# Cross-attention and routed feed-forward on one core: query tiles apart, projections to the last unit, and the output projection of three batches inside the last attention

## The chip, the core and the metric

The kernel runs on one core of a Trainium2 chip. Its engines are TensorE (PE, with its weight loads as PEld), VectorE (DVE), ScalarE (ACT), GpSimd (POOL) and SyncE (SP), each with a queue of its own that is worked off in order; they meet by semaphores. SP and POOL also issue the DMAs. What counts is the device time of one execution in microseconds, as the median of the runs.

## What is computed

Eight batches of 224 rows of 512, with 750 rows of context each. All in fp32.

```python
x = x + attention(layernorm(x), ctx)   # 16 heads of 32, bias on the scores, padding mask
    # q = n @ w_q.T + b_q ; k, v = ctx @ w_k.T + b_k, ctx @ w_v.T + b_v
    # attn = softmax(q k^T * SCALING + attn_bias, masked) ; out = (attn v) @ out_proj_w.T + out_proj_b
n = layernorm(x)
    # dists to 32 prototypes, w = softmax(-dists / t), top_w, top_i = top_k(w, 2), top_w normalised
    # h = B[top_i] n (rank 16) ; y = A[top_i] h + bias[top_i]
x = x + sum(top_w * y)
```

## The kernel before

Two stages, each a block of five queues: `weave` and `finish`.

**weave.** Matmuls of the projections are made in three passes with fp32r halves (hi·hi, lo·hi, hi·lo). A batch of attention has 32 **units**, one for each head and half of the query rows (`w` counts units over all batches, `u` within one, `UB` = 32). In unit `w` TensorE turns the first half of the probabilities (`turn(w, 0)`), makes the scores of unit `w + 2`, and turns the second half (`turn(w, 1)`). VectorE adds the bias and finds the maximum (L727) and copies one half of the turned probabilities (L737), ScalarE makes the exponential (L566) and copies the other half (L575). After every eight units (`u % 8 == 1`) TensorE weighs the values for a group of four heads (L930) and turns the inverse sums (L939); GpSimd has widened these (`widen`, L475). `output` writes the group's attention, SyncE stores it to `attn_t` in DRAM.

Between these pieces stand the projections of the next batch: 14 tiles of keys and values and two of queries, 216 **steps** (matmuls) in all. `step_shares` deals them out over the units up to `last`, in three pieces a unit (before and behind the scores, and behind the second turning), none in a unit that weighs. A tile goes to one of two PSUM banks `acc` in turn, and its first step waits until the tile two before is evacuated, by ScalarE (`high_tile`) and VectorE (`low_tile`). Query tiles use one staging buffer (`query_staging`), which is free when its DMA to DRAM is done. `X_AT` says in which units the normalised x of the next batch is turned by TensorE (L887) into `out_ps`, the bank that also holds the attention's output. GpSimd splits the context into halves (L466, L468).

In batch 7 (the last) nothing is left to project. There GpSimd loads and splits the three matrices of the second stage (`load_weights`, `split_weights`, units `CHUNKS_AT`), and at unit 25 the attended rows of batch 0 (`split_attended`, `add_output_bias`).

**finish.** Per batch: output projection (`project_out`, 24 matmuls of 512 columns into `big`), residual into `x1` (L1265), layer norm (`norm`, `deviation`, `normalise`), transposes (`transpose_y`, L1452), distances to the prototypes, top two and weights (`routing`, `routing_weights`), `down` (48 matmuls of 224 columns), the route widened and transposed (L1186, L1490), `gate`, `up` (24 matmuls) and `result`. A **turn** of its loop holds the second half of batch `b` with the first half of `b + 1` and the projection of `b + 2`. GpSimd splits the attended rows of the next batch and adds the output bias to its x.

## Time and profile before

| | us |
|---|---|
| median of 3 runs | 901.77 (899.92 to 902.45) |
| profiled execution | 899.01 |
| its span, first to last instruction | 896.8 |
| TensorE busy in the span | 848.1 (95%) |
| VectorE, ScalarE, GpSimd busy | 610.3, 502.0, 185.3 |

In the span the first batch's projections come first, with the exponential of the first unit at 52.6 us. Batches then follow every 85 to 86 us until 648.5, where the attention of batch 7 starts. Its last exponential starts at 707.6, the second stage has its first matmul at 714.98, and the last instruction is at 896.8. The mean granted clock of TensorE is 0.992 of full speed. A share of busy time over the whole span mixes these stages, so they are to be read one by one.

### The profile page before, as it was taken

What the parts mean: (1) busy time and instruction counts of PE and PEld (TensorE: products, weight loads), DVE (VectorE), ACT (ScalarE), POOL (GpSimd) and SP (SyncE); (2) the same over time, 40 slices, a digit from 0 to 9 for tenths busy, and PEclk for the clock granted to TensorE, in tenths of its full rate; (3) what the DMA queues carried; (4) which work ended last, traced back from release to release, by engine and by line L of the source; (5) the groups of instructions that cost most, each with busy time, mean ns of one, the idle gap of its engine ahead of it and who ended that gap; (6) DMA issues with size and microseconds to landing.
All of it is one profiled execution on the core that took longest, in us unless ns stands there. A gap on an engine that the chain in (4) does not pass through costs nothing. (4 is left out here: it accounts for less than half of the span.)

```text
span 896.8 us, 20533 instructions
## 1 busy us (share of the span) xinstructions
PE 848.1 (95%) x8016; PEld 751.9 (84%) x8016; DVE 610.3 (68%) x1459; ACT 502.0 (56%) x1066; POOL 185.3 (21%) x240
## 2 busy tenths in 40 slices
PE   6999999999999999999999999999988769999998
PEld 6789898988898889889988989898876647888886
DVE  6586776677666666776686668666678457666664
ACT  5246666665565655666666566666667515444442
POOL 0050112011211201120112011200067233334400
PEclk9999999999999999999999999999999979999999
DMA  8975654675467647565556565546587211222211
GB/s 258 285 161 142 169 148 110 167 173 142 114 165 175 147 110 177 142 143 148 143 134 160 142 155 123 141 108 157 135 200 183 61 51 43 62 62 64 71 30 43
DMA packets 79457, 119.87 MB, mean 134 GB/s; under 512 B 8517, under 2 KB 58797, under 8 KB 79362
## 3 DMA queue, kind: packets, MB, share of 16 engines
q1 hardware_dynamic: 76866, 109.91, 48.8%
q0 software_dynamic: 2496, 8.65, 3.4%
q8 instruction: 64, 1.05, 0.5%
q14 instruction: 31, 0.25, 0.1%
HBM read 79.25 MB, written 39.28 MB: 132 GB/s over the span
## 5 line engine op out<-in xcount | busy, mean ns | idle before, releaser
L566 ACT ACTIVATE score_sb<-score_sb,neg_max 112x750 f32<-112x750 f32 x256 | 236.3, 923 | 74.2 <-DVE neg_max L727 72.4
L727 DVE CUSTOM_DVE_ANT_0 score_sb<-score_ps,neg_bias 112x750 f32<-112x750 f32 x256 | 239.4, 935 | 44.0 <-PE score_ps L906 43.3
L915 PE MATMUL prob_ps<-ident,score_sb 112*125 112x112 f32 x1536 | 248.7, 270 | 8.6 <-ACT score_sb L566 8.0
L915 PEld LDWEIGHTS prob_ps<-ident,score_sb 112*125 112x125 f32 x1536 | 229.9, 188 | 29.7 <-ACT score_sb L566 14.2
L575 ACT ACTIVATE probs_sb<-prob_ps 125x336 f32<-125x336 f32 x256 | 114.7, 448 | 170.5 <-PE prob_ps L915 168.2
L737 DVE COPY probs_sb<-prob_ps 125x336 f32<-125x336 f32 x256 | 129.0, 504 | 117.4 <-PE prob_ps L915 115.2
L902 PE MATMUL score_ps<-k_st,q_st 97*112 97x512 f32 x256 | 105.8, 413 | 0.2 <-DMA q_st<-q_parts 0.2
L475 POOL COPY rsum_wide<-rsum 112x256 f32<-112x256 f32 x32 | 12.7, 398 | 414.9 <-DVE rsum L746 414.9
L861 PE MATMUL acc<-ctx_hi,w_hi 128*128 128x376 f32 (+1 forms) x256 | 88.3, 345 | 7.7 <-DVE ctx_lo L762 7.0
L861 PE MATMUL acc<-ctx_lo,w_hi 128*128 128x376 f32 (+1 forms) x256 | 93.9, 367 | 0.0
L861 PE MATMUL acc<-ctx_hi,w_lo 128*128 128x376 f32 (+1 forms) x256 | 91.1, 356 | 0.0
L869 PE MATMUL acc<-w_hi,ctx_hi 128*125 128x512 f32 x192 | 78.9, 411 | 4.7 <-DVE q_lo L667 4.7
L869 PE MATMUL acc<-w_lo,ctx_hi 128*125 128x512 f32 x192 | 81.9, 427 | 0.0
L930 PE MATMUL out_ps<-probs_sb,v_sb 125*32 125x112 f32 x3072 | 80.2, 260 | 0.6 <-ACT probs_sb L575 0.6
L869 PE MATMUL acc<-w_hi,ctx_lo 128*125 128x512 f32 x192 | 80.3, 418 | 0.0
L906 PE MATMUL score_ps<-k_st,q_st 97*112 97x238 f32 x256 | 71.8, 280 | 5.1 <-DVE neg_max L727 5.0
L930 PEld LDWEIGHTS out_ps<-probs_sb,v_sb 125*32 125x32 f32 x3072 | 72.5, 110 | 4.1 <-issue 0.8
L906 PEld LDWEIGHTS score_ps<-k_st,q_st 97*112 97x112 f32 x256 | 45.1, 176 | 16.9 <-DVE neg_max L727 12.2
L861 PEld LDWEIGHTS acc<-ctx_hi,w_hi 128*128 128x128 f32 x256 | 49.2, 192 | 9.9 <-issue 6.2
L468 POOL TENSOR_TENSOR ctx_lo<-ctx_raw,ctx_hi 128x376 fp32r<-128x376 f32 x56 | 55.6, 993 | 4.7
L861 PEld LDWEIGHTS acc<-ctx_hi,w_lo 128*128 128x128 f32 x256 | 49.3, 193 | 2.8
L861 PEld LDWEIGHTS acc<-ctx_lo,w_hi 128*128 128x128 f32 x256 | 49.3, 193 | 1.9
(165 smaller groups left out, 1484.4 us busy)
## 6 DMA issues: line engine op xcount, KB each, us to landing
k_st<-k_parts SPq DMA_DIRECT2D x96, 375.0 KB
k_parts<-key_parts SPq DMA_DIRECT2D x60, 188.0 KB, 2.3
k_parts<-key_parts SPq DMA_DIRECT2D x60, 187.0 KB, 5.0
q_st<-q_parts SPq DMA_DIRECT2D x96, 112.0 KB
ctx_raw<-in_ctx_t SPq DMA_DIRECT2D x14, 752.0 KB, 6.7
xb<-in_x SPq DMA_DIRECT2D x8, 448.0 KB, 7.2
attn_t<-attn SPq DMA_DIRECT2D x32, 112.0 KB, 1.9
out<-y_out SPq DMA_DIRECT2D x16, 224.0 KB, 2.3
```

The lines of the kernel that those rows point to most:

```text
L468: eng.tensor_tensor(ctx_lo[f][:, k, :], src, ctx_hi[f][:, k, :].bitcast(F32), ALU.subtract)\
L475: eng.tensor_copy(rsum_wide[:, :, :, :], rsum[:, :].rearrange("t (c r) -> t c r", c=TC).unsqueeze(3) .broadcast_to([TW, TC, HG, D])).then_ ...
L566: nc.scalar.activation(scores[:, w % NSC, :], scores[:, w % NSC, :], ACT.Exp, bias=neg_max[:, w % UB:w % UB + 1], scale=-1.0, accum_out=su ...
L575: nc.scalar.activation(probs_sb[q % NPB][0:SW, h * ST + BT:(h + 1) * ST, :], prob_ps[1][0:SW, 0:BT * TW].rearrange("p (s t) -> p s t", s=B ...
L727: nc.vector.tensor_tensor_reduce(out=scores[:, w % NSC, :], in0=score_ps[:, at:at + S], in1=neg_bias[:, w // HG % TC, :], scale=1.0, scala ...
L737: nc.vector.tensor_copy(probs_sb[q % NPB][0:SW, h * ST:h * ST + BT, :], prob_ps[0][0:SW, 0:BT * TW].rearrange("p (s t) -> p s t", s=BT))\
L861: last = nc.tensor.matmul(acc[n % 2][:, 0:SH[f]], w_part[a][1][:, k, g * P:(g + 1) * P], ctx_part[c][f][:, k, K_AT[f]:K_AT[f] + SH[f]], st ...
L869: last = nc.tensor.matmul(acc[n % 2][0:SW, :], ctx_part[c][f][:, k, at:at + SW], w_part[a][2][:, k, :], start=(r == 0), stop=(m == end - 1))
L902: nc.tensor.matmul(score_ps[:, at + main[0]:at + main[1]], q_st[p][:, h, c * TW:(c + 1) * TW], k_st[p][:, h, main[0]:main[1]], start=True, ...
L906: nc.tensor.matmul(score_ps[:, at + mid[0]:at + mid[1]], q_st[p][:, h, c * TW:(c + 1) * TW], k_st[p][:, h, mid[0]:mid[1]], start=True, sto ...
L915: last = nc.tensor.transpose(prob_ps[j][0:SW, s * TW:(s + 1) * TW], scores[:, w % NSC, (BT * j + s) * SW:(BT * j + s + 1) * SW], ident[0:T ...
L930: last = nc.tensor.matmul(out_ps[h * D:(h + 1) * D, c * TW:(c + 1) * TW], v_sb[b % 2][0:SW, s, (g * HG + h) * D:(g * HG + h + 1) * D], pro ...
```

## The change

Four things. (1) The order of a woven batch's tiles: the two query tiles stood next to each other and now have three tiles between them; x is turned one unit later. (2) The steps are dealt out to unit 31 too. (3) The output projection of batches 0, 1 and 2 is made inside the attention of batch 7: four matmuls in each of 18 units, into `acc`, with the residual on VectorE into the values' buffer, which is free by then. For this the weights are split earlier (the output matrix during batch 6, through two stages in `ctx_raw`), and GpSimd and SyncE bring in and split four batches of attended rows in batch 7. Layer norm of batch 0 is made at the end of the block. (4) `finish` starts with batch 0's transposes; its loop projects batch `b + 5` instead of `b + 2`, in three of its turns instead of six, and the norm of `b + 2` stands ahead of the gate's low part, its normalising ahead of the route's weights.

```diff
-CHUNKS_AT = (4, 6, 7, 9, 10, 12, 14, 15, 17, 18, 20, 22)
+CHUNKS_AT = (20, 23, 26, 29, UB + 1, UB + 2, UB + 3, UB + 9, UB + 10, UB + 13, UB + 17, UB + 18)
+EARLY = 3
+OUT_AT = (8, 15, 22)
+OUT_UNITS = tuple(tuple(u for u in range(first, first + 7) if u % UG != 1)[0:6] for first in OUT_AT)
+SPLITS_AT = {5: 0, 11: 1, 19: 2, 26: 3}
+BIASES_AT = {7: 0, 15: 1, 22: 2, 29: 3}
+ATTENDED_AT = {2: 0, 9: 1, 17: 2, 24: 3}
...
-NEXT_TILES[NG + BT:NG + BT] = QUERY_TILES
+NEXT_TILES.insert(NG, QUERY_TILES[0])
+NEXT_TILES.insert(2 * NG, QUERY_TILES[1])
...
-X_AT = (3, 4)
+X_AT = (4, 5)
...
-    last = UB - 1
+    last = UB
...
@@ SyncE
+                if b == B - 1 and u in ATTENDED_AT:
+                    n = ATTENDED_AT[u]
...
+                        eng.wait_ge(sh.at_ready, n)
+                        eng.wait_ge(sh.xb_ready, n)
...
+                    load_attended(eng, sh, x, attn_t, n, sh.at_loaded, sh.xr_loaded)
@@ GpSimd
+                if i >= 2:
+                    eng.wait_ge(wf_lo_done, i - 1)
+                eng.dma_start(wf_stage[i % 2], w_dram[j][k * P:(k + 1) * P, :]).then_inc(wf_loaded[i % 2], 16)
...
+                if b == B - 1 and u in SPLITS_AT:
...
+                    split_attended(eng, sh, at_part[n % 2], sh.at_loaded, n + 1, n, passed)
+                if b == B - 1 and u in BIASES_AT:
...
+                    add_output_bias(eng, sh, sh.xr_loaded, n + 1)
+            root(B)
+            widen(B * NG - 1)
@@ VectorE
+                for n, units in enumerate(OUT_UNITS):
+                    for c in range(TC):
+                        if w == UNITS - UB + units[3 * c + 2] + 1:
+                            residual(n, c)
+                if w in (UNITS - 2, UNITS - 1):
+                    row_stats(w - UNITS + 2)
+                if w == UNITS - 1:
+                    x_variance(B)
+                if w == UNITS:
+                    newton(B)
+                    normalise_rows()
@@ TensorE
+                out = [(n, 4 * units.index(u)) for n, units in enumerate(OUT_UNITS) if b == B - 1 and u in units]
+                for n, step in out:
+                    project_out(n, step, step + 2)
                 if w < UNITS:
                     turn(w, 1)
                 project_steps(b + 1, m[2], m[3])
+                for n, step in out:
+                    project_out(n, step + 2, step + 4)
@@ finish, VectorE, the loop
             for b in range(LAST):
+                ahead = b + EARLY + 2
...
                 routing_dot(b + 1)
+                if b + 2 < B:
+                    norm(b + 2)
                 gated_low(b)
...
+                if ahead < B:
+                    residual(ahead, 1)
                 if b + 2 < B:
                     normalise(b + 2)
+                routing_weights(b + 1)
@@ finish, TensorE
+            transpose_y(0)
             for c in range(TC):
-                project_out(0, c, True)
-            transpose_y(0)
+                project_out(EARLY, c)
             eng.wait_ge(pt_ready, 1)
             distances(0)
-            project_out(1, 0)
+            down(0, 0, 0)
             transpose_dot(0)
...
+                if ahead < B:
+                    project_out(ahead, 0)
```

ScalarE in the seventh attention, where the tiles of batch 7 are evacuated: `q_hi` (in the new kernel a part of `kq_parts`, L586) is a query tile, `kq_parts` at L577 a key tile. Before:

```order
546 L553 ACTIVATE q_hi<-acc,nbq 128x224 x2
547 L566 ACTIVATE score_sb,sums<-score_sb,neg_max 112x750
548 L575 ACTIVATE probs_sb<-prob_ps 125x336
549 L566 ACTIVATE score_sb,sums<-score_sb,neg_max 112x750
550 L575 ACTIVATE probs_sb<-prob_ps 125x336
551 L566 ACTIVATE score_sb,sums<-score_sb,neg_max 112x750
552 L575 ACTIVATE probs_sb<-prob_ps 125x336
553 L553 ACTIVATE q_hi<-acc,nbq 128x224 x2
```

The same place now:

```order
535 L586 ACTIVATE kq_parts<-acc,nbq 128x224 x2
536 L608 ACTIVATE probs_sb<-prob_ps 125x336
537 L599 ACTIVATE score_sb,sums<-score_sb,neg_max 112x750
538 L608 ACTIVATE probs_sb<-prob_ps 125x336
539 L577 ACTIVATE kq_parts<-acc,bias_col 128x376
540 L599 ACTIVATE score_sb,sums<-score_sb,neg_max 112x750
541 L608 ACTIVATE probs_sb<-prob_ps 125x336
542 L599 ACTIVATE score_sb,sums<-score_sb,neg_max 112x750
543 L608 ACTIVATE probs_sb<-prob_ps 125x336
544 L599 ACTIVATE score_sb,sums<-score_sb,neg_max 112x750
545 L608 ACTIVATE probs_sb<-prob_ps 125x336
```

The second query tile followed the first after three units; now key and value tiles stand between them, and it comes eight units later.

TensorE in units 8 and 9 of batch 7: L902, L906 (now L984, L988) are scores, L915 (L997) the turned probabilities, L930 (L1012) the weighing, L961 the output projection. Before:

```order
2718 L902 MATMUL score_ps<-k_st,q_st 112x512
2719 L906 MATMUL score_ps<-k_st,q_st 112x238
2720 L915 MATMUL prob_ps<-ident,score_sb 125x112 x6
2721 L902 MATMUL score_ps<-k_st,q_st 112x512
2722 L906 MATMUL score_ps<-k_st,q_st 112x238
2723 L915 MATMUL prob_ps<-ident,score_sb 125x112 x3
2724 L930 MATMUL out_ps<-probs_sb,v_sb 32x112 x48
2725 L939 MATMUL out_ps<-ident,rsum_wide 128x112 x2
```

Now:

```order
2725 L984 MATMUL score_ps<-k_st,q_st 112x512
2726 L988 MATMUL score_ps<-k_st,q_st 112x238
2727 L961 MATMUL acc<-w_hi,ctx_hi 112x512
2728 L961 MATMUL acc<-w_lo,ctx_hi 112x512
2729 L997 MATMUL prob_ps<-ident,score_sb 125x112 x3
2730 L961 MATMUL acc<-w_hi,ctx_lo 112x512
2731 L961 MATMUL acc<-w_hi,ctx_hi 112x512
2732 L997 MATMUL prob_ps<-ident,score_sb 125x112 x3
2733 L984 MATMUL score_ps<-k_st,q_st 112x512
2734 L988 MATMUL score_ps<-k_st,q_st 112x238
2735 L997 MATMUL prob_ps<-ident,score_sb 125x112 x3
2736 L1012 MATMUL out_ps<-probs_sb,v_second 32x112 x48
```

Unit 8 has gained its four matmuls, two on each side of the second turning; unit 9, which weighs, has none.

TensorE at the border of the two blocks. Before:

```order
2794 L939 MATMUL out_ps<-ident,rsum_wide 128x112 x2
2795 L212 UNCONDITIONAL_BRANCH
2796 L1421 UNCONDITIONAL_BRANCH
2797 L1430 MATMUL big<-w_hi,at_hi 112x512
2798 L1430 MATMUL big<-w_lo,at_hi 112x512
```

Now:

```order
2891 L1021 MATMUL out_ps<-ident,rsum_wide 128x112 x2
2892 L227 UNCONDITIONAL_BRANCH
2893 L1504 UNCONDITIONAL_BRANCH
2894 L1535 MATMUL tr<-ident,ctx_raw 128x112 x8
2895 L1513 MATMUL big<-w_hi,at_hi 112x512
```

The transposes of batch 0 (`ctx_raw` holds its normalised rows) come first, then the projection, which is that of batch 3.

## Rows read from the trace of the kernel before

**Rows 1.** Stretches: us, length, busy by engine (instructions), granted clock, DMA share, GB/s.

```profile
391.15:477.11 85.96, 83.76 (x875) 76.12 (x874) 59.75 (x135) 52.38 (x115) 14.00 (x21) 1.00 0.59 145
648.51:707.60 59.09, 50.38 (x646) 41.58 (x644) 45.21 (x102) 43.72 (x98) 36.81 (x44) 1.00 0.67 167
714.64:751.30 36.66, 25.29 (x136) 20.36 (x136) 21.30 (x63) 12.23 (x25) 9.39 (x9) 0.81 0.14 40
812.32:832.58 20.26, 20.26 (x132) 17.08 (x131) 13.47 (x44) 8.87 (x16) 7.05 (x7) 1.00 0.24 69
```

**Rows 2.** Waits of TensorE in 391.15 to 477.11: us in total, times, longest.

```profile
PE acc L869 <- DVE q_lo L667: 0.9, 1, 0.9
PE out_ps L887 <- DVE attn L751: 0.6, 1, 0.6
PE score_ps L906 <- DVE neg_max L727: 0.6, 1, 0.6
...
PEld score_ps L906 <- DVE neg_max L727: 1.4, 2, 1.0
```

**Rows 3.** Timeline of TensorE in batch 4, one piece: start us, us, instruction.

```profile
400.95 0.48 PE L869 MATMUL acc<-w_hi,ctx_hi 128*125 128x512 f32 x1
401.27 0.40 PE L869 MATMUL acc<-w_hi,ctx_lo 128*125 128x512 f32 x1
401.50 0.39 PE L869 MATMUL acc<-w_lo,ctx_hi 128*125 128x512 f32 x1
```

**Rows 4.** ScalarE's groups of a unit: busy us, mean ns, idle before.

```profile
L566 ACT ACTIVATE score_sb<-score_sb,neg_max 112x750 f32<-112x750 f32 x256 | 236.3, 923 | 74.2 <-DVE neg_max L727 72.4
...
L575 ACT ACTIVATE probs_sb<-prob_ps 125x336 f32<-125x336 f32 x256 | 114.7, 448 | 170.5 <-PE prob_ps L915 168.2
...
L566 ACT ACTIVATION_READ_ACCUMULATOR score_sb<-score_sb,neg_max 112x1 f32 x256 | 48.6, 190 | 0.0
```

**Rows 5.** Timeline of TensorE in batch 7, one unit and the next one's start.

```profile
664.23 0.58 PE L915 MATMUL prob_ps<-ident,score_sb 112*125 112x112 f32 x3 [0.36 <-ACT score_sb L566]
...
664.99 0.48 PE L915 MATMUL prob_ps<-ident,score_sb 112*125 112x112 f32 x3
665.75 0.36 PE L915 MATMUL prob_ps<-ident,score_sb 112*125 112x112 f32 x1 [0.28 <-ACT score_sb L566]
```

**Rows 6.** Timeline of GpSimd in batch 7, two weight chunks in a row.

```profile
662.90 0.63 POOL L488 TENSOR_SCALAR w_hi<-v_sb 128x512 fp32r<-128x512 f32 x1
...
665.80 0.63 POOL L488 TENSOR_SCALAR w_hi<-v_sb 128x512 fp32r<-128x512 f32 x1
```

**Rows 7.** DMA issues in 640 to 740: count, KB each, median us to landing.

```profile
v_sb<-in_fa_t POOLq DMA_DIRECT2D x4, 256.0 KB, 6.1
```

**Rows 8.** The head: a piece of the chain, two timeline rows, ScalarE's table loads.

```profile
714.98 7.37 PE big L1430 x24
...
718.13 0.42 SPq L1111 DMA_DIRECT2D temp_col<-in_temp  x1
...
729.81 1.75 PE L1452 MATMUL tr<-ident,y 112*128 112x112 f32 x8 [7.47 <-DVE y L1280]
...
L1182 ACT ACT_TABLE_LOAD x8 | 10.3, 1283 | 1.1 <-DVE gap L1312 0.9
```

**Rows 9.** GpSimd and VectorE in the head, then `nwt` L62 as ns min/median/max.

```profile
722.56 0.94 POOL L196 TENSOR_SCALAR at_hi<-ctx_raw 128x896 fp32r<-128x896 f32 x1 [7.74 <-PE big L1430]
725.61 2.48 POOL L205 TENSOR_TENSOR xb<-key_parts,bo_row 112x512 f32<-112x512 f32 x2
726.93 1.18 DVE L62 TENSOR_TENSOR nwt<-nwt,veps 112x2 f32<-112x2 f32 x1
...
L62 DVE TENSOR_TENSOR nwt<-nwt,veps x8: 160/161/1184, 726.9 to 865.3; 112x2 f32<-112x2 f32 x8
```

**Rows 10.** Pieces of the chain in one turn of the second stage.

```profile
813.55 2.76 PE big L1430 x12
...
816.53 2.94 PE big L1430 x12
```

293 lines of the change are left out of this document (164 added, 129 removed).

## The prediction

> **What bounds the kernel now.** I read the stretches first [rows 1]. Batch 4's attention, with batch 5's projections woven in, stands for the seven woven batches: TensorE is busy 83.76 of 85.96 us, VectorE 59.75, ScalarE 52.38. TensorE is the limit there. In batch 7's attention nothing is woven: TensorE is busy 50.38 of 59.09 us, and the loop goes by ScalarE, whose unit costs 923 + 190 + 448 ns = 1.56 us [rows 4]; TensorE's unit of 1.52 us, from 664.23 to 665.75, holds waits for ScalarE [rows 5]. The head of the second stage (714.64 to 751.30) is 36.66 us with 25.29 busy at a mean granted clock of 0.81, between the levels 2.4 and 1.2 GHz. After it a batch takes 20.26 us, TensorE busy for all of it, VectorE for 13.47. Six such turns lead to about 873, and the last stretch of nearly 24 us is batch 7's own. So a gain can come from TensorE's waits in the woven batches, its room in batch 7, the head, and matmuls that leave the second stage.
>
> **Query tiles apart, steps to the last unit.** Per woven batch TensorE waits once for q_lo, once for the attention's output ahead of the turning of x, and once for neg_max: 0.9 + 0.6 + 0.6 = 2.1 us on its matmuls, and as a weight load is held longer (1.4 for neg_max), up to 2.9 [rows 2]. The first wait is there because both query tiles use one staging buffer and end three units apart; now it is eight. The second goes as x is turned at units 4 and 5, not 3 and 4. The third stands at the batch's edge, where units 31 and 1 both had no steps and VectorE fell behind TensorE; now unit 31 has eight steps. I take 2.8 in six passes, and 0.5 for the first, which starts fresh: 17.3. Against it, three more pieces a batch: a piece's first matmul starts 0.32 us ahead of the next, the second 0.23 [rows 3], so 3 x 0.09 x 7 = 1.9 us. **15.5 us saved** (9 to 18). What is late next is nobody: VectorE has 26 us a batch to spare.
>
> **Output projection of batches 0 to 2 in batch 7.** 72 matmuls of 512 columns go into 18 units, four each, in two pieces of two. A unit's own TensorE work is 0.76 us to the second group of three transposes and about 0.31 for these, 1.07, with some 0.15 of slack in it that goes when TensorE is never idle [rows 5]. Four matmuls add 2 x (0.32 + 0.23) = 1.10, [rows 3] less some 0.15 (0 to 0.3) as a step overlaps with the transposes ahead of it. 0.92 + 0.95 = 1.87 us against 1.56: 18 x 0.31 = 5.6 us. To this comes the wait of TensorE for the first split. I followed GpSimd from batch 7's start: widening and two weight chunks, 2.9 us each [rows 6], to about 9 us; the third chunk's transfer is issued only when one of two stages is free and lands up to 6.1 us later [rows 7], so it ends near 14; the split takes 3.1 us (722.56 to 725.61, [rows 9]) and ends at 18 with its wait. TensorE reaches unit 8 about 17.7 us in. That is 0.4 us, and the splits of batches 1 and 2 come 5 us or more ahead. Six residual additions on VectorE, 0.3 us over the unit each at worst, mostly fit between. **6.3 us lost** (3 to 12). Statistics, root and normalising of batch 0 lie under the last weighing; the root stands ahead of the last widening on GpSimd, with half a us to spare: 0.2 us lost.
>
> **The head.** Before: 24 matmuls of the projection in 7.37 us, part at the lower clock, then TensorE idle for 7.47 us until y is there, then a second chain of this kind, and 36.66 us until the distances of batch 1 start [rows 1, 8]. Now it starts with batch 0's transposes, the projection of batch 3 covers their evacuation, and that of batch 4 stands behind the down matmuls. The small constants are issued as before, the last 3.5 us in [rows 8], so I have them by 6 to 6.5, with the distances of batch 0 and VectorE's residuals behind them. My count: distances at 7.5 us, down matmuls to 14.4, transposes, projection to 21; there TensorE waits for the route of batch 0 and the residual of batch 4, as VectorE has to do normalise(1), constants, routing, weights, yt and residual: 23.4, plus 0.9 for the route's transposes, 24.2.
> A VectorE instruction on SBUF alone is held up while GpSimd runs one: `nwt` at 726.93 took 1.18 us under the bias addition, against 0.16 for most [rows 9]. In the new order normalise(1) falls under GpSimd's split and bias for batch 4: 2.4 us more; and if the clock drops in the first projection again, up to 1.7. I take 26.5 (24 to 29.5): **10.2 us saved**. Behind that row stands the Trainium skill, SBUF — State Buffer, "SBUF: two separate sides": the pair of ports is held for a whole instruction and the other side fully blocks; by that rule, the trace agrees.
> The ScalarE table loads in this path take 1283 ns each [rows 8]. The Trainium skill, ScalarE: Activation LUTs, "What ACT_TABLE_LOAD costs", speaks against the change here: about 2.66 us for a switch with its drain. By the page two switches would make the head some 2.8 us longer; no row of before shows a drain.
>
> **The second stage from there.** A turn's projection takes 2.76 + 2.94 = 5.70 us of its 20.26 [rows 1, 10]. Three turns keep it (batches 5 to 7), three lose it, which leaves TensorE 14.56. VectorE without its two residuals has some 12.1 us of work. I laid such a turn out: the norm now stands ahead of the gate's low part, the route's weights end 12.4 us in, the widened route 12.9, yt 14.6, just 0.9 before TensorE wants it. So the turn stays TensorE's, with little room: 14.8. 3 x (20.26 - 14.8) = **16.4 us saved** (8 to 17.1).
>
> **Sum.** 896.8 - 15.5 + 6.3 + 0.2 - 10.2 - 16.4 = 861.2 us of span; with the 2.2 us outside it 863.4, against 899.01 of the same execution. The median of the runs before, 901.77, is 0.31% above, so 866.
>
> **Rivals.** (a) The three late turns become VectorE's. For it: a margin of 0.9 us in a chain through four engines. Against it: 12.1 us of work. At 17.5 us a turn it costs 8: 874. Chance 0.15. (b) The waits in the woven batches only move, since TensorE lives there on buffers that others free, and at unit 1 neg_max may be late all the same. Half the saving: 874. Chance 0.12. (c) GpSimd is late in batch 7, as each attended load waits for the bias before it and each chunk for a transfer; the key loads share the DMA engines. A first split 3 to 6 us later: 869 to 872. Chance 0.13. (d) All is hidden better, head 24, turns 14.56, no collision: 857 to 860. Chance 0.10. (e) Slower than before: TensorE runs its queue in order, so a late split stops the attention too, and load, split, matmuls, residual and bias form a ring over four engines. It costs once a ring takes longer than the seven units between two starts, some 15 us. To lose the 36 us gained each of three rings would have to take 27; by the rows it is 6.1 + 3.1 + 2.5 beside the matmuls. Chance 0.02, at 905. (f) The change does not do what it says: the instruction order shows the moves, so what is left of this is (b).
>
> **Chances and range.** The forecast, 861 to 869, has 0.48. Time 866. Range 857 to 876, which takes in (a) to (d) and leaves out (e) and two of them together. A measurement of this kernel tells 0.3% from no change. Faster by more 0.97, within 0.3% 0.01, slower 0.02.
>
> **What would show it.** Woven batches start 83.4 us apart, not 85.7, and the waits for q_lo and attn are gone (first term). Batch 7 takes 65 us, with ScalarE waiting for TensorE in 18 units; a wait of TensorE for at_hi or at_lo at unit 8 of over 2 us is (c). The head has 26 us to batch 1's distances, one wait ahead of the route's transposes, and stretched `nwt` rows. Three turns of 20.3 us follow and three under 15; one over 16 with TensorE waiting for yt or the route is (a). It is wrong altogether if the granted clock falls in batch 7, or if the load of the next batch's first keys comes late, as key tile 4 ends one unit later, two units ahead of it.

## The result, and the profile after

The new kernel takes 878.01 us (876.64 to 878.85, 4 runs) beside 900.89 (899.92 to 902.45, 4 runs) for the kernel before: a ratio of 0.9741, 95% interval 0.9723 to 0.9759. It is faster, as forecast, but 878.0 lies 12 us above the 866 and 2 us outside the range of 857 to 876.

The profiled execution took 878.85 us, its span is 876.4 against 896.8. Cut at the same events in both traces (starts of the exponentials L599; the first issue of `pt_stage` and the first distance matmul of each batch in the second stage), the 20.4 us come from:

| stretch | before | after | change | forecast |
|---|---|---|---|---|
| to the first exponential | 52.6 | 52.8 | +0.2 | 0 |
| seven woven batches | 595.9 | 588.7 | -7.2 | -15.5 |
| batch 7, first to last exponential | 59.1 | 69.3 | +10.2 | +6.3 |
| from there to the first issue of the second stage | 7.2 | 7.3 | +0.1 | +0.2 |
| head, to batch 1's distances | 36.5 | 29.3 | -7.2 | -10.2 |
| six turns | 121.6 | 105.1 | -16.5 | -16.4 |
| tail | 24.0 | 24.0 | 0 | 0 |

The three stretches that missed are 8.3, 3.9 and 3.0 us short of the forecast: 15.2 us, which is the 876.4 measured against the 861.2 forecast. First the stretches of the new kernel, with the columns of [rows 1]: batch 4, batch 7, the head, a turn with a projection and one without.

```profile
387.54:472.18 84.64, 83.95 (x874) 75.94 (x873) 59.52 (x135) 52.25 (x115) 14.03 (x21) 1.00 0.60 149
641.45:710.73 69.28, 64.88 (x726) 56.14 (x725) 48.41 (x109) 44.49 (x100) 39.78 (x40) 0.98 0.60 153
718.03:747.37 29.34, 24.24 (x136) 19.94 (x137) 17.89 (x51) 11.20 (x24) 10.99 (x11) 0.88 0.28 81
747.37:767.67 20.30, 20.30 (x133) 17.10 (x132) 17.48 (x44) 8.98 (x16) 11.79 (x11) 1.00 0.27 77
820.00:834.70 14.70, 14.70 (x107) 13.05 (x106) 11.80 (x41) 8.88 (x18) 0.00 (x0) 1.00 0.11 33
```

Read the first number of busy time beside the length. In the woven batch TensorE is now busy for all but 0.7 us, yet its busy time has grown by 0.2 us, from 83.76 to 83.95, for the same work. In the late turns it is busy for all of it, as forecast. Batch 7 has a granted clock under 1.00, and TensorE is idle there for 4.4 of its 69.3 us.

Waits of TensorE in batch 4, to be held against [rows 2]:

```profile
PEld score_ps L988 <- DVE neg_max L780: 2.3, 5, 0.6
...
PEld out_ps L1021 <- issue: 0.7, 4, 0.2
PE score_ps L988 <- DVE neg_max L780: 0.4, 2, 0.2
PEld out_ps L969 <- DVE at_lo L707: 0.3, 1, 0.3
```

The waits for q_lo and for attn are gone, as forecast. The weight load of the second score matmul now waits for neg_max at five places, not two, 2.3 us instead of 1.4. The other waits of TensorE's weight loads in batch 4 of the kernel before, which belong to [rows 2]:

```profile
PEld acc L869 <- DVE q_lo L667: 1.2, 1, 1.2
PEld out_ps L887 <- DVE attn L751: 0.8, 1, 0.8
...
PEld prob_ps L915 <- ACT score_sb L566: 0.2, 1, 0.2
```

TensorE at the start of batch 7, and the stretches of 2 us there (columns of [rows 1]; the third number from the end is the clock):

```profile
645.33 0.47 PE L984 MATMUL score_ps<-k_st,q_st 97*112 97x512 f32 x1
646.93 0.37 PE L988 MATMUL score_ps<-k_st,q_st 97*112 97x238 f32 x1 [1.14 <-DVE neg_max L780]
647.14 0.48 PE L997 MATMUL prob_ps<-ident,score_sb 112*125 112x112 f32 x3
647.55 4.17 PE L1012 MATMUL out_ps<-probs_sb,v_first 125*32 125x112 f32 x96
```

```profile
645.45:647.45 2.00, 0.86 (x7) 0.54 (x5) 1.85 (x5) 0.81 (x2) 1.85 (x2) 1.00 1.07 221
647.45:649.45 2.00, 2.00 (x50) 1.90 (x52) 0.95 (x2) 1.83 (x5) 1.65 (x3) 0.61 1.04 258
649.45:651.45 2.00, 2.00 (x54) 2.00 (x48) 0.00 (x0) 0.00 (x0) 1.42 (x3) 0.54 0.35 127
651.45:653.45 2.00, 1.97 (x26) 1.59 (x18) 1.02 (x2) 0.37 (x2) 1.88 (x2) 1.00 0.66 172
```

VectorE has a low part to make (L682, 645.42 to 646.03) before it adds the bias, and TensorE waits 1.14 us. Right behind this wait the granted clock falls to half, the lower of its two levels, for over 3 us: the weighing takes 4.17 us, 2.51 at full clock. The wait itself isn't new. The kernel before has it at the same place, behind the same kind of low part, and its clock stayed at full there:

```profile
651.53 0.36 PE L906 MATMUL score_ps<-k_st,q_st 97*112 97x238 f32 x1 [1.14 <-DVE neg_max L727]
```

New is that eight steps of the last tile run over the batch's edge and stand in the first 2.2 us of batch 7, where the kernel before has none. Later in the batch, in the weighing of unit 19:

```profile
681.42 2.31 PE L1012 MATMUL out_ps<-probs_sb,v_second 125*32 125x112 f32 x86
685.15 0.57 PE L1012 MATMUL out_ps<-probs_sb,v_second 125*32 125x112 f32 x10 [1.42 <-issue]
```

"issue" means that TensorE waited for nothing that the profile shows. In the DMA records one 16 KB transfer on an instruction queue starts at 682.19 and takes 1.47 us. Which engine's instructions it brings isn't recorded; more on it under new_again.

### The profile page after: what moved, and what is told of

Same layout as the page of the kernel before. It is cut to its first block and busy times, and to the rows that moved or that the text cites. A ratio compares the mean times of both kernels' runs of the same rounds, so it can differ in the third digit from the quotient of the medians.

```text
span 876.4 us, 20540 instructions
## 1 busy us (share of the span) xinstructions
PE 845.6 (96%) x8016; PEld 751.7 (86%) x8016; DVE 613.9 (70%) x1458; ACT 502.5 (57%) x1065; POOL 183.3 (21%) x237
## 5 line engine op out<-in xcount | busy, mean ns | idle before, releaser
L599 ACT ACTIVATE score_sb<-score_sb,neg_max 112x750 f32<-112x750 f32 x256 | 236.2, 923 | 71.5 <-DVE neg_max L780 68.9
L997 PEld LDWEIGHTS prob_ps<-ident,score_sb 112*125 112x125 f32 x1536 | 233.9, 188 | 20.7 <-ACT score_sb L599 4.4
L997 PE MATMUL prob_ps<-ident,score_sb 112*125 112x112 f32 x1536 | 246.4, 269 | 2.7 <-ACT score_sb L599 2.5
L984 PE MATMUL score_ps<-k_st,q_st 97*112 97x512 f32 x256 | 105.2, 411 | 0.0
L925 PE MATMUL acc<-ctx_hi,w_hi 128*128 128x376 f32 (+1 forms) x256 | 92.2, 360 | 8.2 <-DVE ctx_lo L815 7.4
L925 PE MATMUL acc<-ctx_lo,w_hi 128*128 128x376 f32 (+1 forms) x256 | 91.6, 358 | 0.0
L933 PE MATMUL acc<-w_hi,ctx_hi 128*125 128x512 f32 x192 | 89.5, 466 | 0.0
L988 PE MATMUL score_ps<-k_st,q_st 97*112 97x238 f32 x256 | 73.1, 286 | 5.6 <-DVE neg_max L780 3.9
L933 PE MATMUL acc<-w_lo,ctx_hi 128*125 128x512 f32 x192 | 76.0, 396 | 0.0
L933 PE MATMUL acc<-w_hi,ctx_lo 128*125 128x512 f32 x192 | 75.7, 394 | 0.0
L988 PEld LDWEIGHTS score_ps<-k_st,q_st 97*112 97x112 f32 x256 | 45.1, 176 | 23.5 <-DVE neg_max L780 18.4
L984 PEld LDWEIGHTS score_ps<-k_st,q_st 97*112 97x112 f32 x256 | 44.9, 175 | 4.3 <-issue 0.3
L599 ACT ACTIVATION_READ_ACCUMULATOR score_sb<-score_sb,neg_max 112x1 f32 x256 | 48.5, 190 | 0.0
```

The costliest lines, as they stand in the source:

```text
L599: nc.scalar.activation(scores[:, w % NSC, :], scores[:, w % NSC, :], ACT.Exp, bias=neg_max[:, w % UB:w % UB + 1], scale=-1.0, accum_out=su ...
L925: last = nc.tensor.matmul(acc[n % 2][:, 0:SH[f]], w_part[a][1][:, k, g * P:(g + 1) * P], ctx_part[c][f][:, k, K_AT[f]:K_AT[f] + SH[f]], st ...
L933: last = nc.tensor.matmul(acc[n % 2][0:SW, :], ctx_part[c][f][:, k, at:at + SW], w_part[a][2][:, k, :], start=(r == 0), stop=(m == end - 1))
L984: nc.tensor.matmul(score_ps[:, at + main[0]:at + main[1]], q_st[p][:, h, c * TW:(c + 1) * TW], k_st[p][:, h, main[0]:main[1]], start=True, ...
L988: nc.tensor.matmul(score_ps[:, at + mid[0]:at + mid[1]], q_st[p][:, h, c * TW:(c + 1) * TW], k_st[p][:, h, mid[0]:mid[1]], start=True, sto ...
L997: last = nc.tensor.transpose(prob_ps[j][0:SW, s * TW:(s + 1) * TW], scores[:, w % NSC, (BT * j + s) * SW:(BT * j + s + 1) * SW], ident[0:T ...
```

## The experiments

All of them in one table, from the profiled execution of each: mean of the six woven batches behind the first, batch 7 with its first four units and its unit 19, the head, the first two turns together, and the span. A "half" beside the first four units marks the ones in which the granted clock fell there. The head and the turns hold falls of the granted clock as well, which come at other places in other executions; so the new kernel's own two executions (after, new_again) lie 0.8 us apart in the head and 0.7 in the turns. `b_apart` is the kernel before with one edit; all others are the new kernel with the edits told below.

| | woven | batch 7 | units 0-3 | unit 19 | head | turns 1, 2 | span |
|---|---|---|---|---|---|---|---|
| before | 85.79 | 59.10 | 9.88 | 3.77 | 36.53 | 40.52 | 896.8 |
| after | 84.63 | 69.28 | 12.41 half | 5.83 | 29.34 | 40.56 | 876.4 |
| new_again | 84.70 | 69.19 | 12.35 half | 5.78 | 30.12 | 41.29 | 877.3 |
| b_apart | 85.58 | 60.86 | 11.47 half | 3.77 | 36.64 | 40.58 | 897.4 |
| queries_together | 84.59 | 67.33 | 10.75 | 5.55 | 30.13 | 42.57 | 876.7 |
| last_30 | 85.56 | 68.62 | 9.88 | 6.53 | 29.32 | 40.55 | 882.8 |
| x_at_3 | 85.52 | 67.35 | 10.75 | 5.56 | 27.95 | 42.10 | 881.0 |
| adds_first | 84.80 | 65.48 | 9.65 | 4.04 | 30.89 | 41.40 | 875.0 |
| thin_copies | 84.55 | 67.23 | 10.70 | 5.49 | 29.37 | 40.52 | 873.1 |
| thin_out | 84.65 | 61.42 | 10.75 | 3.77 | 27.82 | 40.55 | 866.7 |
| att_19 | 84.66 | 75.19 | 12.36 half | 6.29 | 30.78 | 41.43 | 885.7 |
| small_loads | 84.77 | 69.81 | 12.41 half | 6.33 | 27.80 | 42.12 | 877.3 |
| small_first | 84.79 | 67.37 | 10.75 | 5.55 | 30.67 | 42.57 | 880.2 |
| no_load_four | 84.64 | 67.63 | 10.74 | 5.83 | 30.92 | 41.12 | 876.6 |
| thin_four | 84.64 | 68.12 | 10.74 | 6.34 | 24.55 | 41.81 | 872.2 |
| two_buffers | 84.69 | 68.99 | 12.38 half | 5.55 | 28.07 | 40.52 | 874.4 |
| bias_late | 84.65 | 68.19 | 10.75 | 6.38 | 25.56 | 42.03 | 874.6 |
| both_head | 84.67 | 68.23 | 10.75 | 6.37 | 26.65 | 43.00 | 876.3 |
| best | 84.80 | 65.32 | 9.65 | 4.04 | 26.46 | 42.99 | 872.5 |
| adds_and_bias | 84.78 | 65.46 | 9.65 | 4.04 | 28.00 | 43.00 | 876.4 |

### The woven batches

**queries_together**: the query tiles next to each other again (and with them the number of tiles after which half of the context is free).

```diff
-NEXT_TILES.insert(NG, QUERY_TILES[0])
-NEXT_TILES.insert(2 * NG, QUERY_TILES[1])
+NEXT_TILES[NG + BT:NG + BT] = QUERY_TILES
...
-HALF_A_TILES = (2 * NG + NG // 2 + 3, 2 * NG)
+HALF_A_TILES = (2 * NG + NG // 2 + 3, NG + 3)
```

> The changed kernel with the old order of tiles, both query tiles in a row. Theory A (each of the three parts removed its own wait, and new ones came by the new places of the tile ends): TensorE's wait for q_lo is back with 0.8 to 1.1 us a woven batch, some neg_max waits of 0.3 us go or come elsewhere; a batch is 84.6 to 85.7 us. Theory B (the query tiles were worth nothing, the other two parts gave the 1.3 us): 84.6 within 0.2.

879.89 us, ratio 0.9761 [0.9705, 0.9817]. A woven batch takes 84.59 us, no more than in the new kernel. Once the steps reach unit 31 and x is turned a unit later, the single staging buffer costs nothing that is left to see.

**b_apart**: the kernel before with the query tiles apart, the same two places edited the other way.

```diff
-NEXT_TILES[NG + BT:NG + BT] = QUERY_TILES
+NEXT_TILES.insert(NG, QUERY_TILES[0])
+NEXT_TILES.insert(2 * NG, QUERY_TILES[1])
...
-HALF_A_TILES = (2 * NG + NG // 2 + 3, NG + 3)
+HALF_A_TILES = (2 * NG + NG // 2 + 3, 2 * NG)
```

> The kernel before with one part of the change alone: the query tiles apart (and the number of tiles after which half of the context is free). Theory A (the wait for q_lo goes and nothing else comes): a woven batch falls from 85.7 to 84.7 us, total 6 to 7 us less, about 0.7%. Theory B (new waits for neg_max take its place, since other tiles now end where VectorE is busy): 85.2 to 85.9 a batch, total within 3 us of before.

899.35 us (10 runs) beside 901.1 (13), ratio 0.9987 [0.9967, 1.0008]: not to be told from no change. Of the 0.9 us that TensorE waited for q_lo [rows 2] a batch gets back 0.2.

**last_30**: steps up to unit 30 only.

```diff
-    last = UB
+    last = UB - 1
```

> The changed kernel with the steps dealt out to unit 30 as before. Theory A (the step-free last unit is what made the wait for neg_max at the batch's edge): one wait of about 1 us is back at each batch's start, the batch is 85 to 85.6 us, and the attention of batch 7 starts with fewer steps in its first units, so it is 1 to 2 us shorter. Theory B (with or without steps in unit 31 the time is the same, since the waits move): 84.6 within 0.3 and other units show the neg_max waits.

**x_at_3**: x turned at units 3 and 4 again.

```diff
-X_AT = (4, 5)
+X_AT = (3, 4)
```

> The changed kernel with x turned in units 3 and 4 as before. Theory A: TensorE's wait for attn ahead of the turning, 0.8 us of a matmul start, is back, the small one for at_lo (0.3 us) goes, and a woven batch is 0.4 to 0.8 us longer than 84.6. Theory B: nothing beyond 0.2 us, as VectorE was the one that was late.

last_30: 885.37 us, 0.9822 [0.9766, 0.9877]; x_at_3: 883.92 us, 0.9806 [0.975, 0.9862]. Undone alone, each makes a woven batch 0.9 us longer, though the two of them with the tiles apart had made it only 1.16 shorter. So they don't add up: whichever is missing, TensorE loses nearly the whole gain. The waits of TensorE in batch 4 of last_30, and behind them those of x_at_3:

```profile
PE out_ps L969 <- DVE at_lo L707: 0.8, 1, 0.8
...
PEld out_ps L1021 <- issue: 0.7, 4, 0.2
PE score_ps L988 <- DVE neg_max L780: 0.6, 1, 0.6
```

```profile
PE out_ps L969 <- DVE attn L804: 0.6, 1, 0.6
...
PEld out_ps L969 <- DVE at_lo L707: 0.3, 1, 0.3
PE score_ps L988 <- DVE neg_max L780: 0.2, 1, 0.2
```

**adds_first**: VectorE adds the bias of unit w + 2 ahead of the low parts that fall in unit w.

```diff
+                if w + 2 < UNITS:
+                    add(w + 2)
                 for tile in ended(w - 1, 1, 2):
                     low_tile(*tile)
-                if w + 2 < UNITS:
-                    add(w + 2)
```

> The changed kernel with one thing moved: in VectorE's queue the addition of the bias for unit w + 2 stands ahead of the low parts of tiles that ended in the unit before, not behind them. Theory A (the waits of the woven batches have moved to the second score matmul, which waits for neg_max because VectorE does a tile's low part of 0.6 to 0.8 us first): these waits, 2.3 us on weight loads in batch 4, go, and a woven batch falls from 84.6 to 83.0 us or less; seven batches, 8 to 14 us less in all, about 866 us. Theory B (TensorE's own work is longer in the new weave, through its additional pieces, and the waits fill slack): a woven batch stays within 0.4 us of 84.6, total 875 to 878. Theory C (tiles are now evacuated too late): waits of TensorE for kq_parts, q_lo or v appear, 0.5 us or more each, and the total is 878 or more.

879.02 us, 0.9759 [0.9714, 0.9804]. In batch 4 the waits for neg_max are all gone, and others stand in their place, so that the batch is no shorter (84.80):

```profile
PEld acc L933 <- DVE v_second L693: 0.8, 2, 0.4
...
PE acc L933 <- DVE v_second L693: 0.5, 2, 0.2
PEld acc L925 <- DVE v_first L693: 0.4, 1, 0.4
PEld acc L941 <- DVE v_second L693: 0.4, 1, 0.4
```

What VectorE makes later is waited for instead: TensorE needs the `acc` bank that VectorE's evacuation of a tile empties.

**thin_copies**: two thirds of VectorE's copy of the turned probabilities left out.

```diff
+                many = BT if w < UB else 1
-                nc.vector.tensor_copy(probs_sb[q % NPB][0:SW, h * ST:h * ST + BT, :],
...
+                nc.vector.tensor_copy(probs_sb[q % NPB][0:SW, h * ST:h * ST + many, :],
...
```

> The new kernel with VectorE's copy of the turned probabilities cut from 336 to 112 columns a row in all batches but the first (so two thirds of that half of the probabilities are stale, and the output is not the reference's). Every wait and every other instruction stays. It takes some 224 columns, about 0.23 us at the rate of the other copies, off VectorE in each of 32 units. Theory A (VectorE is what TensorE waits for in the woven batches, although it has a third of its time free, because its work comes in bunches ahead of neg_max): the five waits of 0.30 to 0.38 us at the second score matmul go, and a woven batch takes 82.9 to 83.6 us instead of 84.6. Theory B (the waits are the price of the order in which two score buffers and two acc banks are handed round, whatever VectorE's load): 84.3 to 84.6, the waits at other places. Batch 7: A 67 to 68 (the wait at its edge goes), B 69.

875.53 us (one run). VectorE has 6.8 us less to do in batch 4, and TensorE waits as before, five times, for 2.2 us:

```profile
386.65:471.18 84.53, 83.96 (x874) 75.94 (x873) 52.69 (x135) 52.20 (x116) 14.02 (x21) 1.00 0.60 150
```

```profile
PEld score_ps L989 <- DVE neg_max L780: 2.2, 5, 0.6
```

Theory A falls: VectorE's load isn't what makes neg_max late. What is left is the addition's own 0.93 us between two score matmuls, wherever TensorE has little to do between them; that reading is argued from the rows, and no run takes the addition away.

### Batch 7

**thin_out**: most of the matmuls of each output projection in batch 7 left out. The expectation counts 22 of 24; the edit keeps the first and the last of each half of 12, so that 20 of 24 go, 60 in all.

```diff
+                    if 0 < r < 3 * NG - 1:
+                        continue
```

> The changed kernel with 22 of 24 matmuls left out of each output projection in batch 7 (the first and the last of each half stay, with all waits, splits, loads and residuals), so that batches 0 to 2 have a partial sum there. It measures what the 66 matmuls cost in batch 7. Theory A (TensorE became the limit in 18 units, 0.31 us each, and the rest of the 10.2 us came from the edge and the pause): batch 7 falls from 69.3 to 63 to 65 us. Theory B (residuals, GpSimd and DMA traffic make most of it): it stays above 67. Theory C (the matmuls fit in the room and cost almost nothing): as B with no change at all.

869.14 us (one run), batch 7 61.42. It is 7.9 us shorter. In this, unit 19 falls by 2.06, to 3.77 as before, and the clock doesn't fall in the first four (1.66), ahead of any of these matmuls. That leaves 4.1 us for 60 matmuls; the 5.6 forecast for 72 make 4.7 for as many.

**att_19**: the attended rows of batch 2 are fetched at unit 19, not 17.

```diff
-ATTENDED_AT = {2: 0, 9: 1, 17: 2, 24: 3}
+ATTENDED_AT = {2: 0, 9: 1, 19: 2, 24: 3}
```

> The changed kernel with the load of batch 2's attended rows issued in unit 19 of batch 7 instead of 17. In the changed kernel TensorE stands still for 1.42 us in the middle of the weighing of units 10 to 17, for nothing that the profile shows, right behind an instruction transfer of 16 KB that took 1.47 us while the DMA engines were full with these 896 KB. Theory A (its instructions come late through this traffic): the pause goes or shrinks under 0.5 us, and batch 7 is 67 to 68 us, not 69.3. Theory B (the pause belongs to the place in the program): it stays at 1.2 to 1.6 us. Either way the split of batch 2 stays early enough, as its projection starts in unit 22.

886.92 us, 0.9853 [0.9802, 0.9904]. The idea that this transfer starved TensorE of instructions falls; the pause is 1.9 us long. And the later split stops the attention:

```profile
PE acc L961 <- POOL ctx_lo L213: 3.8, 1, 3.8
PE prob_ps L997 <- ACT score_sb L599: 2.5, 6, 0.8
PE out_ps L1012 <- issue: 1.9, 1, 1.9
```

The expectation had taken the split for early enough at unit 19; it wasn't. This is rival (c) made on purpose: two units later cost 3.8 us of wait and 5.9 in batch 7. The new kernel itself, without that wait, has less than two units in hand.

**small_loads**: the attended rows and x of batches 1 and 2 cut to 14 and 32 KB.

```diff
+    if few:
+        eng.dma_start(sh.at_in[0:16, 0:1, :], attn_t[b, 0:16, :]...).then_inc(at_loaded, 16)
+        eng.dma_start(sh.x_res[0:16, 0:1, :], x[b, 0:16, :]...).then_inc(xr_loaded, 16)
+        return
```

> The new kernel with the attended rows and x of batches 1 and 2, which SyncE brings in during batch 7, cut to 16 rows of one group (14 and 32 KB instead of 448 KB each; the rest is stale, so the output is not the reference's). Theory A (TensorE's pause in the weighing of unit 19 is its instruction queue running dry, as the transfer that refills it shares the DMA engines with the load at unit 17): the pause of 1.1 to 1.9 us marked issue goes, the 16 KB transfer at that place takes under 1.2 us, and batch 7 takes 65.5 to 67 us instead of 67.3 to 69.3. Theory B (the refill comes late whatever else is transferred, since TensorE takes its instructions faster there than they come): the pause stays at 1.1 us or more, and batch 7 at 67 or more.

879.74 us (one run). Theory A falls: the transfer of instructions at that place takes 1.13 us instead of 1.47, and the pause is longer, 1.9 us. DMA traffic isn't the cause.

**new_again**: the new kernel unchanged.

> The new kernel once more, unchanged. Theory A (the pause in the weighing of unit 19 belongs to this order of the instructions): a row marked issue of 1.1 to 2.0 us, batch 7 at 67.3 to 69.8 us, a median of 876.5 to 878.5 us. Theory B (chance): no such row, batch 7 at 65 to 66.

879.6 us (875.78 to 879.94), ratio 0.9753 [0.9724, 0.9782], 6 runs. Batch 7 repeats to 0.1 us, with its pause (1.4) and its fall of the clock. The head doesn't: 30.12. VectorE reached `pt_lo` 8.7 us behind the first issue instead of 9.5, with GpSimd's split at the same 8.4; `pt_lo` took 0.71 us, but two `nwt` rows 1.25 and 1.22 and `route_st` 2.19, and TensorE waited 5.3 us for the residual behind them.

Taken together: the row marked issue is in all 14 kernels that have the new kernel's order of VectorE's work and all of batch 7's matmuls, 1.1 to 2.0 us long, and in none of the three with the bias added first (adds_first, best, adds_and_bias). It belongs to the order, not to chance. TensorE's own instructions are the same in after and adds_first.

The DMA records say more on this pause. Times in us from the start of unit 19's weighing:

| | 16 KB instruction transfer | pause |
|---|---|---|
| queries_together | 0.92 to 2.04 | 2.31 to 3.45 |
| after | 0.77 to 2.24 | 2.31 to 3.73 |
| small_loads | 1.67 to 2.80 | 2.31 to 4.23 |
| bias_late | 1.08 to 2.69 | 2.31 to 4.28 |
| adds_first | -5.53 to -4.24 | none |
| adds_and_bias | -2.49 to -1.11 | none |

In all 14 the pause starts at the same matmul, 2.31 us in; the transfer starts 0.4 to 1.7 us in, and the pause ends 1.3 to 1.6 us behind the transfer's end, whether it is short or long. In the three without the pause the transfer is over before the weighing starts. (In thin_out, where TensorE's own instructions are others, it starts 1.95 us in and there is no pause.) The queue brings 64 such transfers in the span of the new kernel; TensorE has 16,474 recorded instructions there, 257 to a transfer, and no other engine has over 2,000, so they are most likely TensorE's. So the pause is TensorE waiting for a transfer of instructions that starts too late, as far as times can show it. How VectorE's order sets that start isn't settled.

The wait at the edge is 1.14 us in after and in queries_together alike, and the clock fell behind it in the one and not in the other (the weighing took 4.17 and 2.51 us):

```profile
646.42 0.37 PE L987 MATMUL score_ps<-k_st,q_st 97*112 97x238 f32 x1 [1.14 <-DVE neg_max L779]
646.62 0.48 PE L996 MATMUL prob_ps<-ident,score_sb 112*125 112x112 f32 x3
647.03 2.51 PE L1011 MATMUL out_ps<-probs_sb,v_first 125*32 125x112 f32 x96
```

### The head

VectorE and GpSimd in the head of the new kernel, rows of the timeline:

```profile
727.55 2.08 DVE L1321 TENSOR_TENSOR pt_lo<-pt_stage,pt_hi 128x128 fp32r<-128x128 f32 x1 [5.27 <-ACT bst_hi L1276]
...
732.65 0.78 DVE L60 TENSOR_TENSOR nwt<-rstd 112x2 f32<-112x2 f32 x1
...
742.88 0.23 DVE L1422 CAST route_st<-route 112x128 fp32r<-112x128 f32 x1
743.14 0.29 DVE L1425 TENSOR_TENSOR route_st<-route,route_st 112x128 fp32r<-112x128 f32 x1
```

```profile
726.40 0.93 POOL L211 TENSOR_SCALAR at_hi<-kq_parts 128x896 fp32r<-128x896 f32 x1 [5.48 <-PE big L1513]
727.42 2.07 POOL L213 TENSOR_TENSOR at_lo<-kq_parts,at_hi 128x896 fp32r<-128x896 f32 x1
730.91 2.51 POOL L220 TENSOR_TENSOR xb<-kq_parts,bo_row 112x512 f32<-112x512 f32 x2 [1.43 <-DVE x L1347]
```

`pt_lo` took 2.08 us and ended with GpSimd's `at_lo`. The small constants came late as well: `temp_col` landed after 4.2 us, beside the two attended transfers, and after 2.4 in the kernel before.

**small_first**: GpSimd fetches batch 4's rows only when the small constants are there.

```diff
+            eng.wait_ge(small_loaded, 16 * 7)
             for b in range(EARLY + 1, B):
```

> The changed kernel with one wait more: in the second stage GpSimd issues the load of batch 4's attended rows only when the small constants have landed. Theory A (in the head the constants are late, 4.2 us for the last of them against 2.4 before, because 896 KB of attended rows are moved beside them, and the low part of the prototypes is then held up by GpSimd's split, 2.09 us against 0.27): the constants land some 2 us earlier, the split falls behind pt_lo, and the distances of batch 1 start 26 to 28 us into the stage, not 29.8; total 2 to 4 us less. Theory B (the head is bound by VectorE's and ScalarE's chain in any case): the distances of batch 1 start within 0.7 us of where they did. Theory C: batch 4's split is late instead, TensorE waits for at_lo ahead of its projection, and the head is longer by a us or more.

881.27 us, 0.9785 [0.9748, 0.9823]. `temp_col` landed after 2.4 us and `pt_lo` took 0.29, as hoped, and the head was 1.3 us longer (0.6 against new_again). The collisions had only moved: GpSimd's split and bias addition for batch 4 (729.82 to 737.03) now fell on the `bst` rows (1.32, 2.24 and 1.68 us for 0.68, 0.42 and 0.69), and the next split on `route_st`, 2.19 us for 0.29. TensorE waited 7.4 us for the residual behind these. Its span also holds 1.6 us more at the border and 2.0 more in the first turn, both with a granted clock that fell (0.90 in that turn, with no wait of TensorE), so the longer total isn't the edit's alone.

**no_load_four**: batch 4's transfers left out, its split kept.

```diff
+                if b == EARLY + 1:
+                    return
                 load_attended(eng, sh, x, attn_t, b, at_more_loaded, xr_more_loaded)
```

> The new kernel without the two transfers of batch 4's attended rows and x at the head of the second stage (448 KB each); the rows of batch 3 are split and used once more, so the output of batch 4 is not the reference's. GpSimd's instructions stay, and stand at the same places. Theory A (the small constants are late because they share the DMA engines with these transfers): temp_col lands 2.4 us after its issue and not 4.2, the constants are used 1.5 to 2 us earlier; the head (first transfer of the prototypes to batch 1's distances) takes 27 to 28 us instead of 29.3, if pt_lo then runs ahead of GpSimd's split, and 28.5 to 29.3 if the split still holds it up. Theory B (the constants are late because SyncE issues them after the block's border, and the big transfers take nothing): the head stays at 29.3, temp_col at 4.2.

**thin_four**: its split and bias addition cut to 8 columns as well.

```diff
-    eng.tensor_scalar(hi[:, :, :], sh.at_in, 1.0, 0.0, ALU.mult, ALU.add).then_inc(sh.at_hi_ready, 1)
+    eng.tensor_scalar(hi[:, :, 0:few], sh.at_in[:, :, 0:few], 1.0, 0.0, ALU.mult, ALU.add).then_inc(sh.at_hi_ready, 1)
...
```

> As the kernel without batch 4's transfers, and GpSimd's split and bias addition for batch 4 cut to 8 columns a row as well (the output of batch 4 is not the reference's). Theory A (late constants and VectorE held up by GpSimd together make the head 3 us longer than the 26.5 that were forecast): pt_lo takes 0.3 us instead of 2.1, nwt 0.16, and the head takes 25.5 to 27. Theory B (the head is held by something else, the order of VectorE's work or the granted clock): 28 or more, though pt_lo takes 0.3 us.

878.9 and 874.47 us (one run each). Without the transfers the constants were in after 2.4 us, VectorE got to `pt_lo` 7.4 us behind the first issue instead of 9.5, and the head was longer all the same, 30.92 us: VectorE, now earlier, fell under other instructions of GpSimd. Its rows in no_load_four:

```profile
723.52 0.29 DVE L1325 TENSOR_TENSOR pt_lo<-pt_stage,pt_hi 128x128 fp32r<-128x128 f32 x1 [3.17 <-ACT bst_hi L1280]
...
726.06 1.74 DVE L60 TENSOR_TENSOR nwt<-rstd 112x2 f32<-112x2 f32 x1
727.83 1.21 DVE L62 TENSOR_TENSOR nwt<-nwt,veps 112x2 f32<-112x2 f32 x1
729.08 1.22 DVE L64 TENSOR_SCALAR nwt<-nwt 112x2 f32<-112x2 f32 x1
...
738.19 3.35 DVE L1416 TENSOR_SCALAR pick<-iota,top_f,wt 112x32 f32<-112x32 f32 x4
```

In thin_four, with batch 4's part of GpSimd's work gone too, the head took 24.55 us. Batch 4's preparation costs the head 4.8 us. This isn't collisions alone: in thin_four the constants are in sooner, and the granted clock of the head is 0.99, against 0.88 in after and 0.85 in no_load_four.

**two_buffers**: batch 4's split rows have buffers of their own, and are split while VectorE waits for the constants.

```diff
+        second = [sb("second_hi", [P, KT, T], F32R), sb("second_lo", [P, KT, T], F32R)]
...
-                eng.wait_ge(o_ready, TC * b)
+                if b > EARLY + 1:
+                    eng.wait_ge(o_ready, TC * b)
```

> The new kernel with buffers of its own for batch 4's split rows in the second stage, so that GpSimd splits them as soon as they are there, about 5.5 to 8.6 us after the first small transfer, while VectorE still waits for the small constants. Theory A (the split that falls on pt_lo makes the head long): pt_lo takes 0.3 us instead of 2.1 and the head 27.2 to 27.9 us instead of 29.3; the bias addition may still stretch one nwt row to 0.8. Theory B (the head is bound elsewhere, so a late pt_lo is made good later): 29 to 29.5.

876.75 us, 0.9743 [0.9721, 0.9766]; head 28.07. `pt_lo` took 0.29 us, and the 1.3 us gained are less than the 1.8 of its stretch, because two `nwt` rows (0.94 and 1.20) and `route_st` (1.06) were caught in its place.

**bias_late**: VectorE's steps on the expert bias behind the first gate.

```diff
                 gated_low(b)
+                if b == 0:
+                    bias_later()
...
```

> The new kernel with VectorE's four steps on the expert bias (bst, 0.40 + 0.68 + 0.42 + 0.69 = 2.2 us) moved from ahead of the first routing to behind the first gate's low part; TensorE waits for them only at the last matmul of the first up. Theory A (VectorE's row of instructions from pt_lo to yt is the chain of the head): the head takes 27.0 to 27.4 us instead of 29.3, and the first turn 20.3 to 21 as it takes the 2.2 us in its slack. Theory B (TensorE or ScalarE's routing steps are the chain, and VectorE waits there): the head takes 28.5 or more.

879.55 us, 0.977 [0.9741, 0.98]; head 25.56, 3.8 us shorter for 2.2 us of VectorE's work. So the head is VectorE's chain. The other 1.6 aren't fewer collisions: `pt_lo` (0.80) and two `nwt` rows (1.25 and 1.21) are stretched by 2.6 us in all, `pt_lo` and `nwt` in after by 2.4. VectorE reached `pt_lo` 0.9 us sooner, and the granted clock was 0.93, not 0.88. Of the 3.8, 1.5 came back in the next two turns.

**both_head** has both edits, **best** the edit of adds_first besides, **adds_and_bias** bias_late and adds_first alone.

> The new kernel with both changes of the head: buffers of its own for batch 4's split, and the expert bias behind the first gate. Theory A (one chain of VectorE, and both are on it): the savings add up, the head takes 25.0 to 25.8 us and the time is 4 us under the new kernel's, 873 to 875. Theory B (the one covers the other): 27 us. A collision that moves to another instruction of VectorE (a nwt row or the routing stretched by the bias addition) would leave it at 26 to 27.

> The kernel with both changes of the head and VectorE's bias addition of unit w + 2 ahead of the low parts of unit w - 1. Theory A (the order of VectorE's work decides whether TensorE's pause in the weighing of unit 19 occurs): no row marked issue in batch 7, which takes 65.4 to 65.8 us, and a time of 869 to 872. Theory B (chance): a pause of 1.1 to 1.9 us again, batch 7 at 67 to 69, and a time of 872 to 875.

> The new kernel with VectorE's bias addition of unit w + 2 ahead of the low parts of unit w - 1, and its four steps on the expert bias behind the first gate. From the single runs: batch 7 without the pause saves 3 to 4 us, the woven batches lose 6 x 0.15 = 0.9, the head saves up to 3.8 of which 1.5 is given back in the first two turns: a span of 871 to 872.5 and a median of 872 to 875. Theory A (the parts are independent): this. Theory B (the earlier start of the second stage moves GpSimd's split onto another instruction of VectorE, so the head's part is lost): 874 to 877, with the head at 27 us or more or the first turn over 22.

both_head: 878.04 us, 0.9749 [0.9728, 0.977]; best: 877.11 us (874.68 to 882.72), 0.9751 [0.9712, 0.979]; adds_and_bias: 878.65 us (875.54 to 882.50), 0.975 [0.9717, 0.9784]. The head's parts don't add up: in both_head batch 5's split starts 25.5 us behind the first issue, and head and two turns together take 69.65 us, as in the new kernel (69.90), where bias_late alone had 67.59; new_again had 71.41, so a difference of 1.5 us here is within what one kernel shows. Batch 7 is 65.3 to 65.5 us in each kernel with the bias added first. But the intervals of all of them and of the new kernel overlap, so none is shown to be faster. The executions of adds_and_bias lie 7 us apart, the shortest at a mean granted clock of 0.998 and the longest at 0.989.

## Why the prediction was right or wrong

**The woven batches** (15.5 forecast, 7.2 measured) are the largest error, and the step that failed is "what is late next is nobody". It was reasoned from VectorE's 26 free us a batch. thin_copies gave VectorE 7 more, and nothing came of it. The waits that were named did go, but TensorE's weight loads were held for 3.6 us a batch before ([rows 2] and the rows beside the result, without those on issue: 1.4 + 1.2 + 0.8 + 0.2) and for 2.6 after (2.3 + 0.3). That is 1.0 us, and the batch got 1.16. Rival (b) is what happened, and at half the saving it was priced nearly right. The subtraction for three more pieces does no harm and isn't seen: TensorE's busy time grew by 0.2 us a batch, where 0.27 was taken. b_apart, last_30 and x_at_3 show the same from the other side: 0.2, 0.9 and 0.9 for single parts that make 1.16 together. (The term's own sum, 17.3 - 1.9, is 15.4.)

**Batch 7** (+6.3 forecast, +10.2 measured). The term for the matmuls was right: outside the first four units and unit 19 the batch is 5.6 us longer than before, and 5.6 was forecast; the units with four matmuls that don't weigh take 1.8 to 1.9 us (1.87 forecast). The step that failed is that the sum had no term for what lies outside them. Three things make up the rest. The eight steps over the batch's edge cost 0.9 us (10.75 for 9.88 in the first four units). A fall of the clock there costs 1.66; it isn't shown to be the change's own: the kernel before has the same wait without the fall, b_apart the wait with it (11.47 for 9.88), and queries_together, with the whole change but the tiles' order, the wait without it (10.75). And unit 19 costs 2.1 (5.83 for 3.77), 1.8 of it the pause (4.04 with the bias added first). The two forecast terms of 0.4 and 0.3 didn't show: TensorE came to unit 8 late enough for the first split, so rival (c) didn't come; where the bias was added first, it came sooner and waited 0.3 to 0.5 us for this split. Those kernels take 65.3 to 65.5 us, where 65.4 was forecast; that the eight steps don't show in them is luck of their order, in which the wait of 1.14 us is gone. The prediction held a fall of the clock in this batch for a sign of being wrong altogether; it came, and cost 1.66 us.

**The head** (-10.2 forecast, -7.2 measured). The count of TensorE's and VectorE's steps was right: 24.2 us without collisions, 24.55 measured in thin_four. The term for collisions was mis-sized: 2.4 us, where everything above the 24.55 is 4.8 to 6.4 (29.34 and 30.12 in two executions of the same kernel, 30.92 without the transfers). This holds the constants' delay and the falls of the clock too, which no run parts from the collisions. Two steps failed. The constants were taken as in by 6 to 6.5 us, "issued as before"; beside the attended transfers the last landed 8.6 us in (7.8 in new_again), and 6.5 in no_load_four. And the collision was placed on normalise(1) alone, while it fell on `pt_lo`, `bst`, `nwt`, `pick` or `route_st`, whichever stood at that moment. Behind these rows stands the Trainium skill, SBUF — State Buffer, "SBUF: two separate sides", whose rule of full blocking the trace bears out: `pt_lo` ends 0.14 us behind `at_lo`. What the page can't give is the moment. The dearer table switches that the prediction weighed did not come: in the new head a load takes 1.28 us and the next activation starts 0.01 us behind it (728.15 and 729.44).

**The turns** (-16.4 forecast, -16.5 measured) were right to a tenth: three of 20.3 and three of 14.74, TensorE busy throughout. The three late ones are 14.74 in all 18 kernels that have them, so rival (a) didn't come. The tenth is luck in the first: it took 20.99 in new_again (granted clock 0.96) and 22.28 in queries_together (0.90), with no wait of TensorE. Border and tail were right as well.

The direction was right, and so was the sign of each term. The range failed because the cases of error were added up as rivals to each other, one at a time, while (b), a worse head and a worse batch 7 came together: 8.3 + 3.0 + 3.9. It isn't one unlucky measurement: of the ten runs of the new kernel (four and, in new_again, six) one, 875.78, lies in the range.

## What to carry to other kernels

When an engine is within 3% of always busy, look at who frees its buffers unit by unit, not at how much free time its neighbours have: a wait that is taken away comes back at the next hand-over, and parts that each cost 0.9 us when undone may bring only 1.2 together. Before a stretch that is one chain of VectorE, lay GpSimd's instructions from SBUF beside it on one time axis, and take their whole length as the stretch. Where several terms of a sum can each fall short, let the range hold two of them at once. And when one part of an execution got longer, look at the granted clock of that part before blaming the edit.
